# Head choice without a DRAM round trip, and an earlier transpose in the rotary attention

## The reference, cut to what matters

```python
dist = softmax(mean(x @ Wr + br, axis=1), axis=-1)          # 8 x 16
top_vals, top_idx = top_k(dist, 4)
g = take_along_axis(softmax(sparse(top_vals), axis=1), top_idx, axis=1)
Qk, Kk, Vk = [take(x @ W + b, top_idx) * g for W, b in ((Wq,bq),(Wk,bk),(Wv,bv))]
out = softmax(Qk @ Kk.T / 8) @ Vk;  return out @ Wo + bo
```

```python
q, k = apply_rope(q), apply_rope(k)
out = softmax(where(causal, q @ k.T * 64**-0.5, min)) @ v;  return out @ w_out.T
```

## Time and profile before

| | us |
|---|---|
| time, median of 3 (least to greatest) | 3835.32 (3834.57 to 3835.72) |
| the profiled execution's own time | 3842.36 |
| its span | 3840.4 |
| its mean granted TensorE clock, share of full | 0.743 |
| busy PE, PE weight load, DVE, ACT, POOL | 3163.6, 2402.2, 2258.7, 1695.6, 1211.7 |
| head choice, first issue to the first work of `attention_core` | 1588.67 to 1627.74 |

### The profile page before, as it was taken

One profiled execution on the slowest core, in us unless ns is written; L12 is line 12 of the kernel. 1 busy time (PEld: TensorE's weight loads), 2 busy tenths in 40 slices (PEclk: granted clock), 3 DMA queues, 4 the chain that ended last, 5 costly groups with the idle time before them and its releaser, 6 DMA issues. The chain is left out here.

```text
span 3840.4 us, 143685 instructions
## 1 busy us (share of the span) xinstructions
PE 3163.6 (82%) x58952; PEld 2402.2 (63%) x58952; DVE 2258.7 (59%) x6772; ACT 1695.6 (44%) x5164; POOL 1211.7 (32%) x1528
## 2 busy tenths in 40 slices
PE   8677488988889888489985899999999889999571
PEld 5445188888888888445532566666666567777451
DVE  4667644444444444368865888889888845555232
ACT  2179333333333333257743555565555534444230
POOL 0032410000000000033310655565555544444332
PEclk9899755555555555589997999999999955555786
DMA  4011100000000000010001000000000010110336
GB/s 132 1 55 46 31 25 14 25 14 14 25 14 25 14 14 25 13 34 21 20 1 52 2 3 3 2 3 3 2 3 2 16 50 31 33 33 28 109 97 173
DMA packets 112984, 116.09 MB, mean 30 GB/s; under 512 B 55041, under 2 KB 96458, under 8 KB 112371
## 3 DMA queue, kind: packets, MB, share of 16 engines
q1 hardware_dynamic: 104674, 87.36, 8.0%
q0 software_dynamic: 7824, 21.46, 1.5%
HBM read 79.65 MB, written 29.13 MB: 28 GB/s over the span
## 5 line engine op out<-in xcount | busy, mean ns | idle before, releaser
L676 PE MATMUL banks<-hp,whp 128*128 128x8 f16 x24576 | 741.4, 168 | 118.3 <-DVE hp L743 118.3
L676 PEld LDWEIGHTS banks<-hp,whp 128*128 128x128 f16 x24576 | 697.7, 104 | 179.1 <-DVE hp L743 170.2
L709 ACT ACTIVATE ig<-banks 128x32 f32<-128x32 f32 x512 | 101.4, 198 | 576.8 <-PE banks L676 576.8
L738 DVE SCALAR_TENSOR_TENSOR carry<-ig 128x16 f32<-128x16 f32 x512 | 92.1, 180 | 425.4 <-ACT ig L709 425.4
L646 POOL COPY HT<-hist 128x128 f32 x64 | 21.3, 408 | 987.0 <-DVE hp L748 987.0
L1747 PE MATMUL rnn_banks<-rnn_hp,rnn_whp 128*128 128x8 f16 x6144 | 285.6, 171 | 41.1 <-ACT rnn_hp L1805 15.6
L1747 PEld LDWEIGHTS rnn_banks<-rnn_hp,rnn_whp 128*128 128x128 f16 x6144 | 247.8, 107 | 108.3 <-ACT rnn_hp L1805 76.6
L1088 ACT ACTIVATE att_PH<-att_stp 128x1024 f16<-128x1024 f32 (+3 forms) x258 | 183.4, 711 | 296.6 <-PE att_stp L888 296.6
L1147 POOL TENSOR_TENSOR att_QK<-att_rot,att_QK 128x512 f16<-128x512 f32 x133 | 187.4, 1409 | 244.1 <-ACT att_QK L1080 244.1
L654 PE MATMUL banks<-xs,wxp 128*128 128x64 f16 x3168 | 263.7, 241 | 0.0
L1007 DVE TENSOR_TENSOR att_PL<-att_P,att_PH 128x1024 f16<-128x1024 f32 (+3 forms) x257 | 236.0, 957 | 0.5 <-issue 0.2
(11 more groups left out here) (595 smaller groups left out, 7767.1 us busy)
## 6 DMA issues: line engine op xcount, KB each, us to landing
gen_w<-in_L_cond_W_dram SPq DMA_DIRECT2D x32, 512.0 KB
exp_xt<-expert_rows_scratch SPq DMA_DIRECT2D x80, 129.0 KB
edge_cb<-cols_scratch SPq DMA_DIRECT2D x16, 512.0 KB, 3.7
XT<-expert_found_scratch SPq DMA_DIRECT2D x16, 512.0 KB, 5.0
mod_xn<-in_x_dram SPq DMA_DIRECT2D x8, 512.0 KB
XT<-in_xT_dram SPq DMA_DIRECT2D x1, 4096.0 KB
out_dram<-exp_ob SPq DMA_DIRECT2D x64, 64.0 KB, 2.2
attw_st<-in_L_attn_w_qkvT_dram SPq DMA_DIRECT2D x6, 512.0 KB
```

The costliest lines, as they stand in the source:

```text
L676: last=nc.tensor.matmul(out, whp[:,wpart,k,col:col+128], hp[:,k,hpart], start=False,stop=True,skip_group_check=True)
```

## The change

The DRAM tensors, their six transfers and their semaphores go. DVE writes two small diagonal tiles on 8 partitions, each index or gate in the block of its own sequence and zero elsewhere. A product of PE with a matrix of ones adds up the 8 partitions, and so leaves all 32 values on all 128 partitions of a PSUM bank. For the gates there are two products, added up, whose matrices have ones in one half of the columns. DVE copies row 0 of the index product to `idx`, compares directly with the product in PSUM, and copies the gates. The cast of `heads` moves ahead of the wait for the logits. POOL fills the matrices (`all_one`, 8 x 128, and `halves`, 8 x 2 x 128). `own_heads` is 8 x (8 x 4), `own_gates` 8 x 2 x (8 x 2). In the rotary slot of PE, `turn_outputs` moves from behind the second group of scores to ahead of it.

```diff
             def rope_slot(it,s):
...
                 project(it,2*(s+2)+1)
+                if s>=1: turn_outputs(it,s-1)
                 if s>=-1: scores(it,s+1,1)
-                if s>=1: turn_outputs(it,s-1)
                 if s>=0: scores_T(it,s,1)
...
+    pl,ph,pg=[c1.enter_context(nc.psum_tensor("pick_"+n,[P,512],F32)) for n in ("l","ph","pg")]
...
             def _(sp):
-                sp.wait_ge(dv,8)
-                sp.dma_start(i_dram,ti[:,0:K0].bitcast(I32)).then_inc(heads_out,16)
-                sp.wait_ge(dv,12)
-                sp.dma_start(g_dram,g[:,:]).then_inc(gates_out,16)
-                sp.wait_ge(heads_out,16)
-                sp.dma_start(idx[:,:],i_dram.rearrange("(a b) k -> a (b k)",a=1)).then_inc(picked,16)
-                sp.dma_start(idb[:,:],i_dram.rearrange("(a b) k -> a (b k)",a=1).broadcast_to([P,NB*K0])).then_inc(spread,16)
-                sp.wait_ge(gates_out,16)
-                for h in range(2):
-                    sp.dma_start(gate[h*DH:(h+1)*DH,:,:],g_dram.rearrange("b (n h) -> h b n",h=2)[h:h+1].broadcast_to([DH,NB,NP0])).then_inc(bl,16)
-                sp.wait_ge(picked,16)
+                sp.wait_ge(picked,1)
                 load_heads(sp,0,lambda kk: slice(kk,kk+1))
-                sp.wait_ge(bl,32)
                 sp.wait_ge(ldb,32)
             def _(pool):
+                nc.gpsimd.memset(all_one[:,:],1.0)
+                for h in range(2):
+                    nc.gpsimd.memset(halves[:,h,h*DH:(h+1)*DH],1.0)
+                    i=nc.gpsimd.memset(halves[:,h,(1-h)*DH:(2-h)*DH],0.0)
             def _(pe):
+                pe.wait_ge(dv,11)
+                nc.tensor.matmul(ph[:,0:NB*K0],all_one[:,:],own_heads[:,:,:].rearrange("p b k -> p (b k)"),start=True,stop=True).then_inc(heads_spread,1)
+                pe.wait_ge(dv,15)
+                for h in range(2): i=nc.tensor.matmul(pg[:,0:NB*NP0],halves[:,h],own_gates[:,h].rearrange("p b n -> p (b n)"),start=(h==0),stop=(h==1))
+                i.then_inc(gates_spread,1)
             def _(dve):
+                dve.wait_ge(ids,3)
+                nc.vector.tensor_copy(heads[:,:,:],heads_i[:,:,:])
                 dve.wait_ge(lgd,1)
...
                 step(nc.vector.tensor_scalar(sc[:,2:3],top[:,0:1],-1.0,None,ALU.mult))
+                step(nc.vector.tensor_copy(tif[:,:],ti[:,0:K0]))
+                step(nc.vector.tensor_tensor(own_heads[:,:,:],eye.broadcast_to([NB,NB,K0]),tif[:,:].rearrange("p (b k) -> p b k",b=1).broadcast_to([NB,NB,K0]),ALU.mult))
+                dve.wait_ge(heads_spread,1)
+                nc.vector.tensor_copy(idx[:,:],ph[0:1,0:NB*K0]).then_inc(picked,1)
                 dve.wait_ge(ex,3)
...
-                dve.wait_ge(ids,3); dve.wait_ge(spread,16)
-                nc.vector.tensor_copy(heads[:,:,:],heads_i[:,:,:])
-                step(nc.vector.tensor_copy(idf[:,:],idb[:,:]))
+                for h in range(2): i=nc.vector.tensor_tensor(own_gates[:,h],eye.broadcast_to([NB,NB,NP0]),g[:,:].rearrange("p (b n h) -> p h b n",b=1,h=2)[:,h].broadcast_to([NB,NB,NP0]),ALU.mult)
+                step(i)
...
-                dve.wait_ge(bl,32)
+                dve.wait_ge(gates_spread,1)
+                step(nc.vector.tensor_copy(gate[:,:,:],pg[:,0:NB*NP0].rearrange("p (b n) -> p b n",b=NB)))
                 step(nc.vector.tensor_tensor(gated_bias[:,:,:],bias[:,:,2,:],gate[:,:,:],ALU.mult))
```

More of the change, by code:

```diff
@@ L1281, in rope_table, with ffn0_stage @@
     return np.ascontiguousarray(np.concatenate([one,one],0))
-def ffn0_stage(nc, XT, HT, Wq,Wk,Wv,Wr,br,Wo,bo, bt, ident, g_dram, i_dram):
+def ffn0_stage(nc, XT, HT, Wq,Wk,Wv,Wr,br,Wo,bo, bt, ident):
     with ExitStack() as ctx:
@@ L1303, in ffn0_stage @@
             sem=c1.enter_context(semaphores(nc,"pick_"))
-            wr=sb1("wr",[P,2,H0]); brs=sb1("br",[1,H0]); one=sb1("one",[1,NB]); hm=sb1("hm",[P,2,NB]); lg=sb1("lg",[NB,H0]); heads_i=sb1("heads_i",[P,NB*K0,H0],I32); heads=sb1("heads",[P,NB*K0,H0]); idb=sb1("idb",[P,NB*K0],I32); idf=sb1("idf",[P,NB*K0]); is_head=sb1("is_head",[P,NB*K0,H0]); term=sb1("term",[P,3,NB*K0,H0]); junk=sb1("junk",[P,BA,T]); sc=sb1("sc",[NB,8]); dist=sb1("dist",[NB,H0]); top=sb1("top",[NB,8]); ti=sb1("ti",[NB,8],U32); e4=sb1("e4",[NB,K0]); g=sb1("g",[NB,K0])
-            pl=c1.enter_context(nc.psum_tensor("pick_l",[P,512],F32))
-            ld,ldb,ids,mean,half_mean,lgd,dv,ex,heads_out,gates_out,picked,bl,spread=[sem(n) for n in "ld,ldb,ids,mean,half_mean,lgd,dv,ex,heads_out,gates_out,picked,bl,spread".split(",")]
+            wr=sb1("wr",[P,2,H0]); brs=sb1("br",[1,H0]); one=sb1("one",[1,NB]); hm=sb1("hm",[P,2,NB]); lg=sb1("lg",[NB,H0]); heads_i=sb1("heads_i",[P,NB*K0,H0],I32); heads=sb1("heads",[P,NB*K0,H0]); tif=sb1("tif",[NB,K0]); own_heads=sb1("own_heads",[NB,NB,K0]); own_gates=sb1("own_gates",[NB,2,NB,NP0]); halves=sb1("halves",[NB,2,P]); all_one=sb1("all_one",[NB,P]); is_head=sb1("is_head",[P,NB*K0,H0]); term=sb1("term",[P,3,NB*K0,H0]); junk=sb1("junk",[P,BA,T]); sc=sb1("sc",[NB,8]); dist=sb1("dist",[NB,H0]); top=sb1("top",[NB,8]); ti=sb1("ti",[NB,8],U32); e4=sb1("e4",[NB,K0]); g=sb1("g",[NB,K0])
+            pl,ph,pg=[c1.enter_context(nc.psum_tensor("pick_"+n,[P,512],F32)) for n in ("l","ph","pg")]
+            ld,ldb,ids,mean,half_mean,lgd,dv,ex,heads_spread,gates_spread,picked=[sem(n) for n in "ld,ldb,ids,mean,half_mean,lgd,dv,ex,heads_spread,gates_spread,picked".split(",")]
             block=c1.enter_context(nc.Block())
@@ L1332, in _ @@
                 nc.gpsimd.memset(one[:,:],1.0).then_inc(ids,1)
-                nc.gpsimd.memset(ones[:,:],1.0).then_inc(ids,1)
+                nc.gpsimd.memset(ones[:,:],1.0)
+                nc.gpsimd.memset(all_one[:,:],1.0)
+                for h in range(2):
+                    nc.gpsimd.memset(halves[:,h,h*DH:(h+1)*DH],1.0)
+                    i=nc.gpsimd.memset(halves[:,h,(1-h)*DH:(2-h)*DH],0.0)
+                i.then_inc(ids,1)
                 nc.gpsimd.iota(heads_i[:,:,:],pattern=[[0,NB*K0],[1,H0]],base=0,channel_multiplier=0).then_inc(ids,1)
@@ L1339, in _ @@
                 nc.tensor.matmul(pl[0:NB,0:H0],one[:,:],brs[:,:],start=False,stop=True).then_inc(lgd,1)
+                pe.wait_ge(ids,2)
+                pe.wait_ge(dv,11)
[3 more added lines that the diff above has]
+                i.then_inc(gates_spread,1)
             @block.scalar
@@ L1369, in _ @@
                 step(nc.vector.tensor_scalar(sc[:,2:3],top[:,0:1],-1.0,None,ALU.mult))
+                eye=ident[0:NB,0:NB].rearrange("p (b k) -> p b k",k=1)
+                step(nc.vector.tensor_copy(tif[:,:],ti[:,0:K0]))
+                step(nc.vector.tensor_tensor(own_heads[:,:,:],eye.broadcast_to([NB,NB,K0]),tif[:,:].rearrange("p (b k) -> p b k",b=1).broadcast_to([NB,NB,K0]),ALU.mult))
+                dve.wait_ge(heads_spread,1)
+                nc.vector.tensor_copy(idx[:,:],ph[0:1,0:NB*K0]).then_inc(picked,1)
                 dve.wait_ge(ex,3)
@@ L1373, in _ @@
                 step(nc.vector.tensor_scalar(g[:,:],e4[:,:],sc[:,6:7],None,ALU.mult))
-                dve.wait_ge(ids,3); dve.wait_ge(spread,16)
-                nc.vector.tensor_copy(heads[:,:,:],heads_i[:,:,:])
-                step(nc.vector.tensor_copy(idf[:,:],idb[:,:]))
-                step(nc.vector.tensor_tensor(is_head[:,:,:],heads[:,:,:],idf[:,:].rearrange("p (a b) -> p a b",b=1).broadcast_to([P,NB*K0,H0]),ALU.is_equal))
+                for h in range(2): i=nc.vector.tensor_tensor(own_gates[:,h],eye.broadcast_to([NB,NB,NP0]),g[:,:].rearrange("p (b n h) -> p h b n",b=1,h=2)[:,h].broadcast_to([NB,NB,NP0]),ALU.mult)
+                step(i)
+                step(nc.vector.tensor_tensor(is_head[:,:,:],heads[:,:,:],ph[:,0:NB*K0].rearrange("p (a b) -> p a b",b=1).broadcast_to([P,NB*K0,H0]),ALU.is_equal))
                 for q in range(3): i=nc.vector.tensor_tensor(term[:,q],is_head[:,:,:],bt[:,q:q+1].broadcast_to([P,NB*K0,H0]),ALU.mult)
@@ L2184, in build @@
         taps_dram=nc.dram_tensor("taps_scratch",[LH,P,P-1+WIN],F32).ap(); cols_dram=nc.dram_tensor("cols_scratch",[EDGES],F16).ap()
-        g_dram=nc.dram_tensor("gates_scratch",[NB,K0],F32).ap(); i_dram=nc.dram_tensor("picked_scratch",[NB,K0],mybir.dt.int32).ap()
         rows_dram=nc.dram_tensor("expert_rows_scratch",[NE*(NB*T+2*P)+2*P,D+2],mybir.dt.int32).ap(); found_dram=nc.dram_tensor("expert_found_scratch",[2*NB*T+2*NE*P,D],F32).ap()
@@ L2213, in build @@
         soon.close()
-        ffn0_stage(nc,XT,HT,*[a["L0_ffn_"+n] for n in ("Wq","Wk","Wv","Wr","br","Wo","bo")],g["bt"],ident,g_dram,i_dram)
+        ffn0_stage(nc,XT,HT,*[a["L0_ffn_"+n] for n in ("Wq","Wk","Wv","Wr","br","Wo","bo")],g["bt"],ident)
         cond1_stage(nc,XT,HT,g)
```

## The result

3806.9 us (3804.16 to 3808.59, four runs) against 3834.95 (3834.14 to 3835.72): the ratio is 0.9927, 95% interval 0.9913 to 0.9942, or 28 us less. I had forecast 3819.7 with a range of 3808 to 3831. The direction was right, and the size was outside the range: 28 where I had 15.6.

The account below looks back on a forecast made before the run. SP's weight issues, stalled behind the gates' tiny packets, were taken to set the head choice's end. Head choice -15.6, transposes 0, clock 0: 3835.32 - 15.6 = 3819.7 us, range 3808 to 3831.

Parts of the forecast that it names:

- the jam of 2048 elements: Head choice: the gates' 4-byte elements, 9.3 ns each, about 19 us, stall the weight issues queued behind them.
- the free pattern of the issues: Head choice: without the gates' packets, SP issues four heads' weights in 3 x 2.16 + 1.40 = 7.9 us.
- The indices' way: Head choice: `idx` about 1599.25 after 1.21 us of added steps, first weight issue at 1600.5, 2.55 earlier.
- The rival that the weights stall by themselves: Head choice: first issues after a pause are slow anyway, only the indices' 2.55 us are won, 3832.8; chance 0.08.
- I keep 3.73, as the last loads have to land either way: From SP's end to `attention_core`: gap kept at 3.73 us; up to 2.9 more gained if the backlog made it.
- Nothing on the cycle moves. Value 0 over 63 slots: Rotary attention: moving the transposes ahead of the second scores gains 0 us; bounds -14 and +6.
- the sign of being wrong: Prediction wrong if 2 us issues stay, DVE ends last in the head choice, or rotary slots change by over 0.1 us.
- the slower rival: Rotary slot: POOL's subtraction holds a further DVE operation, 0.8 x 63 = 50 us slower, net 3870; chance 0.07.
- more gain than forecast: Rival: DVE's 0.23 wait goes in most slots, or the backlog leaves the stage boundary: 3806 to 3812; chance 0.06.
- DVE's 0.23: Rotary slot: DVE's wait for PE's projection, 0.23 us; 63 x 0.23 = -14 if it went altogether.
- Move by 0.1 at most: Rotary slot: transposed scores, exponentials and POOL's work shift by 0.1 us at most, as two PE blocks only swap places.
- 4 us either way: Attention over the chosen heads: TensorE's 1.2 GHz stretches may move with the earlier start; 4 us allowed, nothing counted.

Follow-up runs that it names:

- the three kernels on the gates: Kernel before, gates read as 128-byte rows: ratio 0.9961; changed kernel, gates through DRAM by the two 4-byte transfers: 0.9969; kernel before, gate transfers behind the weights: 1.0015.
- SP's tail: Changed kernel with four more 16 KB transfers and a wait for them at the end of SP's part of the head choice: 3812.63 us.

## Why the prediction was right or wrong

*The head choice, its working.* Right: SP's queue, the jam of 2048 elements, the free pattern of the issues. The indices' way (2.60 against 2.61), the twelve issues (7.97 against 7.9), and DVE's end ahead of SP's by 2.6 (I had 2.3) came as worked out. That the indices' way came out to 0.01 us is luck: `idx` was ready 1.58 after the start of DVE's step and not 1.36, since the way over PE took 0.86 and not 0.59, and from there to the first weight issue it was 1.02 and not 1.26. The rival that the weights stall by themselves is refuted by the three kernels on the gates. The rule of the Trainium skill that I weighed, "DMA: Bandwidth & Descriptors", on the anatomy of one DMA (2.0 us and bytes over 436e3), is given for GpSimd's path and does not carry over to these transfers from SP: for the two, 8 KB together, the runs show 21 us, ten times as much.

*The boundary.* The step that failed is "I keep 3.73, as the last loads have to land either way". It measured 1.06, 2.67 less. That this could come was in my bounds (up to 2.9), and the value taken was wrong, and its reason too: nobody waits for the loads there, only `attention_core` does. After, 442 packets of them move between 1606.1 and 1607.0 and the last at 1607.29, behind the start of the next stage; and with the gates behind the weights no load was under way any more from 1631.7 on, and yet the gap lasted 3.76 us. In the gap of before one packet of the instruction queue (q14) is seen between 1624.1 and 1627.7; after, two lie between 1600 and 1606.1, beside the weights' issues, and none behind SP's end. DMA view of the gap of before (packets, MB, share), then two rows of after, of the gap and of the stretch ahead of it:

```profile
q1 hardware_dynamic: 575, 0.14, 17.0%
q14 instruction: 1, 0.01, 0.5%
```

```profile
q1 hardware_dynamic: 442, 0.11, 52.2%
```

```profile
q14 instruction: 2, 0.02, 0.9%
```

That the wait for this load makes the difference is only argued. It fits the thirteen traces: in the six with such a packet in the gap the next stage begins 2.9 to 3.8 us after the last issue or the last DVE step, and 1.5 to 1.8 after that packet; in the six without one and without a wait for a landing, 1.06 to 1.12 after whichever of SP and DVE was last. (The thirteenth is SP's tail, which waits for its own transfers.) But no run took the load away, so the cause of the 2.67 stays open.

*The transposes.* The step that failed is "Nothing on the cycle moves. Value 0 over 63 slots". It holds for the slot that I had read, to 0.01 us. It fails as I took that one slot for all 64: eight slots, those in which POOL also splits a new batch's tokens, had a stall of their own, 0.98 us each, far above the 0.1 that I had named as the sign of being wrong. The term of the sum that I had put at 0 was worth 7.1 us. I had priced the same mechanism with the other sign (L997's 1.22, on which POOL held DVE), as the slower rival, and gave more gain than forecast a chance of 0.06. That rival's 3806 to 3812 holds the measured time, but not by its reasons: DVE's 0.23 is still there after, and the shorter boundary is not shown to be a backlog's. The Trainium skill, "SBUF — State Buffer", "Who interferes with whom", says that the one that issues first holds the pair; the rows of the race agree with it at distances of 0.07 and 0.01 us, on either side. It also moved a stall in the usual slots: L997 fell from 0.67 us on average to 0.17, and the 128 x 776 form of L1007 ahead of it grew from 1.35 to 1.82, with the slot unchanged.

*"Move by 0.1 at most".* Counted from the slot's second L979, the one in the rows shown, ACT's conversion L1080 behind these exponentials came after 2.95 us instead of 3.18 in usual slots, and instead of 3.33 in the eight, so 0.23 and 0.38 earlier: more than my bound. (Of the 0.22 on PE in the slot shown, 0.10 is that the transposes start sooner behind the projection than the scores did, and 0.12 that the two blocks take 0.82 and not 0.94.) But the subtraction that races is the slot's second L1147, and that one did not move: 8.80 to 8.81 after L979 in all eight slots, before and after. What moved is DVE. Its first L1007, beside the first L1147, took 1.51 to 1.52 us instead of 1.58 to 1.61, and L1010 was issued 8.78 to 8.79 after L979 instead of 8.85 to 8.87. So 0.07 us on DVE's side decided it; that the earlier first L1147 gave them is how I read it, and no run moved that one alone.

*The clock.* I allowed 4 us either way and counted 0. The traces show the stage over the chosen heads in two groups: 18 to 19 us at 1.2 GHz with 308.1 to 308.8 in all, and 27 to 29 with 311.3 to 312.6, with one between. Both groups have old and new head choices, so the 2.5 us of this pair of profiles are not shown to be the change's. With the boundary and the transposes at their measured values the sum would have been 15.6 + 2.7 + 7.1 = 25.4 of the 28.

## What to carry to other kernels

Read a transfer's element size before its bytes: 8 KB in 4-byte pieces held a queue for 21 us, and everything issued behind it too, which the trace shows as slow issues of innocent transfers. Reshaping such a transfer into rows got 15.1 of the 18.2 us here. In a pipelined loop, look at the slots that differ (every eighth here) before multiplying one slot's answer by their number, and treat an operation of 0.15 us that at times takes 1.1 as a race whose outcome any move of 0.1 us may flip. Then issue the small operation well ahead of the other engine's, and not just ahead of it.

## What the runs showed of the hardware that I had not expected

The 2 x 1024 elements of 4 bytes took 9.3 ns each, at 4.7% of the sixteen DMA engines' time, and behind them the issue of a transfer of 64 KB took up to 2.4 us instead of 0.4. A DVE subtraction of 4 x 8 numbers issued 0.07 us behind a POOL subtraction of 128 x 512 ended with that one, 1.13 us; issued 0.01 us ahead of it, it took 0.15 and POOL was not slower (1.18 against 1.17). DVE lost such a race 8 times in one kernel, never in another, and 4 times, in other slots, in a third with the same code in that stage as the second. Over ten traces it lost whenever it was issued 0.014 us or more behind, and never at 0.011 or less.
